# Five warm-up products of 128 columns in place of two of 320 at the head of TensorE's program

## The reference, cut to what matters

```python
x = x + 0.5 * mix(n(x))          # token shift, sigmoid gate, squared ReLU
x = x + t5_attention(n(x))       # 16 heads of 64, relative position bias
x = x + 0.5 * mix(n(x))
x = x + 0.5 * local_layers(n(x)) # 2 layers: windowed attention, gated GELU
x = x + min_gru(n(x))            # scan over time
x = x + 0.5 * local_layers(n(x))
```

## Time and profile before

| | us |
|---|---|
| three timed runs | 1187.62, 1181.19, 1187.14 |
| their median | 1187.14 |
| span of the profiled execution, first to last instruction | 1183.1 |
| the profiled execution's own time | not given by the profile |
| TensorE busy with matmuls | 1131.5 |
| TensorE busy with weight loads | 688.8 |
| VectorE busy | 911.6 |
| ScalarE busy | 919.9 |
| GpSimd busy | 618.1 |

### The profile page before, as it was taken

One profiled execution on the slowest core, in us unless ns is written; L12 is line 12 of the kernel. 1 busy time (PEld: TensorE's weight loads), 2 busy tenths in 40 slices (PEclk: granted clock), 3 DMA queues, 4 the chain that ended last, 5 costly groups with the idle time before them and its releaser, 6 DMA issues.

```text
span 1183.1 us, 39854 instructions
## 1 busy us (share of the span) xinstructions
PE 1131.5 (96%) x15754; PEld 688.8 (58%) x15754; DVE 911.6 (77%) x2423; ACT 919.9 (78%) x2451; POOL 618.1 (52%) x406
## 2 busy tenths in 40 slices
PE   8899999999999998999999999988999899999987
PEld 3365556555556653676666666554556566666664
DVE  5788989888989978877677777767777777777763
ACT  6777878777878777977788787776869778877874
POOL 4456666665656644655465455343453445645540
PEclk9899999999999999999999999999999999999999
DMA  8411111111111123111021011011010101111110
GB/s 274 163 38 39 57 39 56 39 56 39 50 46 47 49 85 99 43 34 42 19 50 42 19 41 34 19 33 36 15 41 19 42 19 42 42 41 29 33 42 19
DMA packets 30361, 58.31 MB, mean 49 GB/s; under 512 B 5680, under 2 KB 7152, under 8 KB 30176
## 3 DMA queue, kind: packets, MB, share of 16 engines
q1 hardware_dynamic: 30176, 55.77, 17.5%
HBM read 15.32 MB, written 1.11 MB: 14 GB/s over the span
## 4 chain that ended last, share of the span: by engine, by line
PE 82%; ACT 6%; DVE 4%; issue 4%; DMA 2%; POOL 1%; SPq 1%; DVEq 0%; ACTq 0%; POOLq 0%
PE ps L312 11%; PE ps L289 10%; PE ps L1453 7%; PE ps L1416 5%; PE ps L1383 5%; PE ps L1353 5%; PE ps L1332 4%; PE ps L1322 4%; PE ps L1423 4%; PE ps L1395 4%; PE ps L1323 3%; PE ps L322 3%; PE ps L1459 2%; PE ps L260 2%; PE ps L266 2%
## 5 line engine op out<-in xcount | busy, mean ns | idle before, releaser
L241 POOL TENSOR_TENSOR arena<-arena 128x1024 f32<-128x1024 f32 x128 | 241.1, 1893 | 152.7 <-DVE arena L520 152.7
L416 ACT ACTIVATE arena<-arena 128x512 f32<-128x512 f32 x256 | 182.4, 713 | 80.8 <-DVE arena L506 80.4
L1264 POOL TENSOR_TENSOR arena<-arena 128x1024 f32<-128x1024 f32 x64 | 121.4, 1896 | 230.5 <-DVE arena L1836 230.5
L1658 ACT ACTIVATE arena<-arena 128x128 f32<-128x128 f32 x512 | 198.2, 390 | 30.2 <-DVE arena L1828 29.6
L506 DVE CUSTOM_DVE_ANT_0 arena<-ps,arena 128x512 f32<-128x512 f32 x256 | 164.3, 688 | 31.4 <-PE ps L289 29.0
L1828 DVE CUSTOM_DVE_ANT_0 arena<-ps,near,arena 128x128 f32<-128x128 f32 x512 | 144.4, 346 | 40.9 <-PE ps L1383 40.9
L516 DVE STREAM_TRANSPOSE arena<-arena 128x1024 f32<-128x1024 f32 x128 | 157.8, 1234 | 1.1 <-POOL arena L241 0.9
L312 PEld LDWEIGHTS ps<-arena 32*64 32x64 f32 x8192 | 119.1, 130 | 56.3 <-issue 55.2
L1271 POOL TENSOR_TENSOR arena<-arena 128x1024 f32<-128x1024 f32 x64 | 151.0, 2360 | 0.1
L312 PE MATMUL ps<-arena 32*64 32x128 f32 x8192 | 136.0, 274 | 6.3 <-issue 6.0
L289 PE MATMUL ps<-arena 64*128 64x512 f32 x512 | 138.4, 633 | 2.0 <-DVE arena L506 1.4
(11 more groups left out here) (161 smaller groups left out, 2148.3 us busy)
## 6 DMA issues: line engine op xcount, KB each, us to landing
arena<-arena SPq DMA_DIRECT2D x127, 128.0 KB, 2.4
arena<-arena SPq DMA_DIRECT2D x64, 192.0 KB, 2.6
arena<-rel_rows SPq DMA_DIRECT2D x16, 448.0 KB, 9.2
arena<-arena SPq DMA_DIRECT2D x64, 64.0 KB, 2.1
arena<-y SPq DMA_DIRECT2D x30, 128.0 KB, 2.3
arena<-arena SPq DMA_DIRECT2D x15, 127.8 KB, 2.4
arena<-in_wqkv SPq DMA_DIRECT2D x2, 768.0 KB, 5.2
x<-in_x SPq DMA_DIRECT2D x4, 256.0 KB, 4.7
```

The lines of the kernel that those rows point to most:

```text
L241: nc.gpsimd.tensor_tensor(e, e, scale, ALU.mult).then_inc(self.normed, 1)
L416: nc.scalar.activation(self.e[:, r % 3, i, :], self.neg[:, i, :], ACT.Exp, bias=self.nmax[:, i:i + 1], scale=-1.0, accum_out=self.sums[:, ...
L1658: nc.scalar.activation(self.e[:, s, h, :], self.neg[:, h, :], ACT.Exp, bias=self.nmax[:, h:h + 1], scale=-1.0, accum_out=self.sums[:, s, h ...
```

## The change

The constant `WARM` becomes 5, a constant `WARM_COLS` of 128 is added, and both the moving operand and the output of the warm-up product are cut to it. The stationary operand, the bank, the wait ahead of the loop and all the rest of the program stay as they are.

```diff
-WARM = 2
+WARM, WARM_COLS = 5, 128
...
             def _(pe):
                 pe.wait_ge(prepared, 2)
                 for _ in range(WARM):
-                    nc.tensor.matmul(k.ps[:, 7, 0:320], k.y[:, B, 1:1 + P], k.y[:, B, 1:1 + 320], start=True, stop=True)
+                    nc.tensor.matmul(k.ps[:, 7, 0:WARM_COLS], k.y[:, B, 1:1 + P], k.y[:, B, 1:1 + WARM_COLS], start=True, stop=True)
                 ahead.pe(pe)
```

## The result

Six runs of the changed kernel take 1190.93 to 1194.99 us, median 1193.45; six runs of the kernel before 1181.19 to 1187.62, median 1186.61. The ratio is 1.0063 with an interval of 1.0045 to 1.0082. The forecast of 1187.1 and its range up to 1190.2 were wrong.

A forecast was written before the change was run, and what follows sets the result against it. The prediction took the tensor engine (96% busy) to bound the kernel and the DMA of `x` its first microseconds; 0.00 + 0.00 us left the median of 1187.1 us, range 1180.5 to 1190.2.

The forecast's parts named there:

- The warm-up's length: Head, L2078: ten passes end at 4.04 against 3.98 us; the 0.06 us growth hides in the wait for `x`, 0.00 us.
- rival A: Warm-up in the head: the weight loads come into the open; +2.0 us, 1189.1 us, chance 0.04.
- The clock in the head: Head from L614 on: equal columns leave the clock's rise where it was; 0 us, bounds -0.7 and +2.6 us.
- rival C: L621 and L165, 8.7 to 11.4 us: the clock rises later; at most 2.6 us, 1189.7 us, chance 0.08.
- Rival D: Past the head: half-clock stretches come or go, so measurement shows something else; 1181 to 1188 us, chance 0.10.
- B: Head, L614: the clock rises earlier because ten passes look busier than four; -0.7 us, 1186.4 us, chance 0.12.
- The step that failed: Memory and queues, TensorE's queue in the head: twelve added instructions issue while the engine would wait, adding no wait.

The follow-up runs named there:

- Experiment 1: Kernel before, old warm-up kept, with three one-column products behind it (12 more instructions); 1189.83 against 1183.65 us, ratio 1.0061.
- Experiment 4: Kernel before with three one-column products (12 instructions) ahead of the last output projection of the T5 attention; ratio 1.0017.
- experiment 2: Kernel before with its two warm-up products cut from 320 to 128 columns, instruction count unchanged; ratio 1.0011.
- Experiment 3: Changed kernel with 13 one-column products behind its warm-up, together 64 instructions more than the kernel before; 1184.01 us, ratio 1.0010.

## Why the prediction was wrong, point by point

**The warm-up's length: right.** The prediction had 0.218 us per pass, an end at 4.04, and a wait for `x` left over. Measured: 2.50 us for ten passes, end at 3.98, 0.62 us of wait. From the second (1.86) on, the ten passes start 0.21 us apart, while the record of one load lasts 0.333 us in the median: the loads are hidden here as at L1353. So rival A did not come true: with the ten loads in the open L614 would have started near 6.9, and it starts at 4.61.

**The clock in the head: right within its bounds, and small.** In the kernel before, the first L621 pass lasts 0.59 us and starts at 8.54. In the profile after, it starts at 8.69 and still lasts 1.06 us, as L266 does where the clock column says 0.50 (1061 ns); the chain of waits has

```profile
8.90 1.42 PE ps L621 x2
```

in place of 0.87 us, and 0.74 us are lost by the first L260: 0.55 us are this pair, and 0.19 us are the wait for block 1 of `x`, which lands at 6.78 and holds the third and fourth pass of L614 back. That is a part of rival C, at about a fifth of its price of 2.6 us. It is not tied to the change. Experiment 1 has the instructions and the loss of the change and reaches its first L260 at 32.60, before the kernel before does. Experiment 4 has the head of the kernel before, instruction for instruction (its lines stand three further down, L624 is L621 and L260 is the same), and its chain has

```profile
8.98 1.71 PE ps L624 x2
33.54 0.86 PE ps L260 x2
```

That is rival C's sign, 1.7 us, with no edit in the head, and 0.83 us lost by the first L260. So the head's length varies by that much between executions, and a difference of 1 us there, as in experiment 2, cannot be put down to an edit from one profile. No run shows the 2.6 us in the upper end of the range. They were the author's estimate: two passes of L621 and four of L165, each 0.43 us longer, half of the 0.86 us that an L260 pair takes. The most that the 14 profiles show is what experiment 4 has: 1.71 in place of 0.87 us for the L621 pair, and 2.25 in place of 1.88 us for the four passes of L165. Behind the attention, the windows of the changed kernel show two half-clock stretches where the kernel before has 1.00 in the same column:

```profile
784.70:788.10 3.40, 3.40 (x13) 2.36 (x11) 1.21 (x5) 1.44 (x6) 0.19 (x1) 0.50 0.35 80
1153.40:1156.70 3.30, 3.30 (x12) 2.16 (x11) 0.49 (x2) 2.15 (x10) 0.90 (x1) 0.50 0.00 0
```

The kernel before has one at 510 that the changed one lacks. Not both of its stretches come after idle time on TensorE: ahead of that at 52.7 the engine stands still for 1.44 us, but ahead of that at 510 the timeline has no idle time, only 24 passes of one column (L927, 2.80 us from 507.54). Rival D was right that such stretches come and go between executions; it was wrong that they are what decides here. Experiment 3 has both of the changed kernel's stretches, about 11 us earlier, and no loss clear of its interval:

```profile
774.00:777.40 3.40, 3.29 (x10) 2.44 (x11) 1.62 (x9) 1.61 (x7) 0.60 (x1) 0.50 0.37 84
1142.70:1146.00 3.30, 3.30 (x12) 2.16 (x11) 0.49 (x2) 2.13 (x9) 0.80 (x1) 0.50 0.00 2
```

One comparison in D was wrong as written: the spread of 6.4 us is nine times B's 0.7 us, but only 2.5 times C's 2.6 us, so it is not "nine times any term above".

**The step that failed** is this sentence: "Twelve more instructions go in ahead of 31,508 on this queue: 0.04%, and they issue while the engine would wait." It priced their own execution, which is indeed free, and took the rest of the program to be untouched: "The rest of the kernel sees the warm-up only through what it does to the clock." In fact all 32,000 instructions behind them moved by 12 against the borders of the 256-instruction blocks in which, as far as the traces show, they are fetched, and one border came to lie in front of the second pass of L289. The term of the sum that was 0.00 is 8.2 us in the profiled execution, the slowest of six, and 0.6% or about 7 us in the timed runs.

**What I had in hand and did not read.** The rows were there in the kernel before: the page's "q8 instruction: 125, 2.05", and the wait list, which for 60 to 430 us says

```profile
PE ps L312 <- issue: 6.0, 5, 1.3
```

Five gaps of up to 1.3 us in the densest line of the kernel, waiting for nothing, are the very thing that moving code can multiply. I read only the first 62 us of the chain. In the changed kernel the same list has 7.3 us in 6 gaps there, and 0.7 us at L289, which had none:

```profile
PE ps L312 <- issue: 7.3, 6, 1.3
PE ps L289 <- issue: 0.7, 2, 0.4
```

The list shows only a part of the loss, since a modelled matmul end covers the beginning of a gap; the unit lengths show it in full.

**What stays open.** What sets the moment at which a block is asked for: in most blocks its packet starts within 1.3 us of the border before, ahead of 243 and 255 often 4.4 to 6.6 us behind it, and this is what decides whether such a border stalls in a round of four units (5 of 7 before) and why 231 and 239 did not. That the late block is an instruction fetch is inferred from the place, the number, the size and the times of the packets; no run changed the fetch itself without moving code. The 1.1 us behind the attention are not taken apart further. Each kernel has one profile, so how the excess varies between executions of one kernel is not known.

## What to carry to other kernels

When an edit adds or removes instructions in a long unrolled program, price the shift of all the code behind it as well as the instructions: look for "issue" gaps in the densest line, find their place in the count of instructions (here 191 or 192 modulo 256 for 93 gaps), and see onto what the borders move. Before a small gain or loss of an edit is put down to its idea, run the old version with the same number of idle instructions added; here that one control gave the whole result. Trying a few such paddings, up to a period, is cheap, and a change should be judged at its best padding.

## What the runs showed of the hardware that I had not expected

- By the count (125 for 32,229 recorded instructions), the size and the times of the packets, TensorE's program seems to come in 16.4 KB packets of 256 instructions; at a border the engine stood still for up to 1.8 us, and the last packet had started 2.2 to 3.0 us before the end of each of 93 gaps.
- The 256 instructions from 307 to 563 of a unit run in 2.03 us, less than that: in the changed kernel the border at 563 had a gap in all seven rounds.
- A shift by 12 instructions costs 0.61%, by 56 nothing measurable (0.9992), by 64, the distance between the borders' places in a unit of 576, nothing measurable either (1.0010).
- A pass of one column with a 32x16 stationary takes about 0.03 us (26 passes in 0.85 us, in the head of experiment 3, where the four L614 passes behind them take 3.75 us): a cheap way to move code.
- In this program two products of 320 columns as a warm-up are worth 0.13% (interval from -0.03% to 0.30%), with their 8 instructions' shift included.
